# The output projection of a gated cross-attention block: one float32 matmul a product, or three in float32r

## What is computed

```python
qh, kh, vh = proj_heads(q, Wq), proj_heads(k, Wk), proj_heads(v, Wv)   # 16 heads of 64, INNER = 1024
scores = einsum('bhqd,bhkd->bhqk', qh, kh) + attn_mask
probs = softmax(scores)
ctx = einsum('bhqk,bhkd->bhqd', probs, vh).transpose(0, 2, 1, 3).reshape(b, s, -1)
attn = einsum('bse,de->bsd', ctx, Wo)                                  # the output projection
x = x + tanh(g_xattn) * attn
x = x + tanh(g_ffn) * ffn(layernorm(x))
```

## Time and profile before

| | us |
|---|---|
| median of 3 runs | 215.25 (215.03 to 215.96) |
| span of the profiled execution | 213.1 |
| TensorE matmuls busy | 198.2 (93%) |
| VectorE busy | 155.0 (73%) |
| ScalarE busy | 104.7 (49%) |
| POOL busy | 70.2 (33%) |

### The profile page before, as it was taken

The page is one execution under the profiler, slowest core; times in us unless marked ns, Lnnn a source line. Parts: engine busy times, 40 slices in busy tenths (PEclk is TensorE's granted clock), DMA queues, the critical chain, the costliest instruction groups (busy, mean ns, idle before and its releaser), DMA issues.

```text
span 213.1 us, 5086 instructions
## 1 busy us (share of the span) xinstructions
PE 198.2 (93%) x1564; PEld 172.4 (81%) x1564; DVE 155.0 (73%) x666; ACT 104.7 (49%) x352; POOL 70.2 (33%) x91
## 2 busy tenths in 40 slices
PE   7766899999989999899996999999999999999994
PEld 8564678987779877798775988888988899888894
DVE  3469998569995699956999587699665556564554
ACT  4354699467674775747757351732223232223230
POOL 3387369633036231362313610131413031230000
PEclk9999999999999999999999799999999999999999
DMA  3890000000000000020000000002202102020002
GB/s 123 288 362 7 3 14 3 12 3 14 0 0 12 0 12 0 0 62 0 0 0 6 0 0 0 5 0 77 74 0 74 59 19 74 0 74 25 0 0 98
DMA packets 5983, 7.99 MB, mean 37 GB/s; under 512 B 817, under 2 KB 3521, under 8 KB 5969
## 3 DMA queue, kind: packets, MB, share of 16 engines
q1 hardware_dynamic: 5904, 7.74, 10.8%
q0 software_dynamic: 64, 0.07, 0.2%
HBM read 7.29 MB, written 0.52 MB: 37 GB/s over the span
## 4 chain that ended last, share of the span: by engine, by line
PE 58%; DVE 21%; issue 7%; ACT 6%; DMA 3%; POOL 2%; DVEq 1%; SPq 1%; ACTq 0%
PE proj_k L397 6%; PE proj_q L397 6%; ACT probs L515 5%; PE misc L303 5%; PE o_bank L294 4%; DVE probs L690 3%; PE pt L225 3%; PE pt L227 3%; PE pt L226 3%; DMA wk_raw<-wkT 3%; PE s_even L269 3%; PE pt L279 3%; PE proj_q L225 3%; DVE rstd L745 3%; PE proj_k L225 2%
## 5 line engine op out<-in xcount | busy, mean ns | idle before, releaser
L515 ACT ACTIVATE probs<-probs,negmax 128x128 f32<-128x128 f32 x128 | 49.9, 393 | 17.6 <-DVE negmax L690 17.6
L1026 POOL TENSOR_TENSOR probs<-probs,rinv 128x512 f32<-128x512 f32 x32 | 33.0, 1042 | 58.0 <-DVE rinv L704 57.8
L592 ACT ACTIVATE silu_sb<-s_even 128x512 f32<-128x512 f32 x18 | 10.8, 598 | 43.8 <-PE s_odd L227 43.8
L515 ACT ACTIVATION_READ_ACCUMULATOR probs<-probs,negmax 128x1 f32 x128 | 24.2, 189 | 0.0
L294 PE MATMUL o_bank<-probsT,v 128*64 128x128 f32 x256 | 17.5, 278 | 3.4 <-DVE probsT L708 1.9
L858 DVE TENSOR_TENSOR h_sb<-silu_sb,s_odd 128x512 f32<-128x512 f32 x18 | 12.3, 685 | 10.7 <-ACT silu_sb L592 10.6
L858 DVE TENSOR_TENSOR h_sb<-silu_sb,pt 128x512 f32<-128x512 f32 x18 | 12.4, 687 | 10.4 <-ACT silu_sb L592 10.3
L294 PEld LDWEIGHTS o_bank<-probsT,v 128*64 128x64 f32 x256 | 13.8, 136 | 7.3 <-issue 6.8
L269 PE MATMUL s_even<-kT,qT 64*128 64x128 f32 x128 | 18.4, 284 | 0.3 <-DVE negmax L690 0.2
L279 PE MATMUL pt<-ident_sb,probs 128*128 128x128 f32 x128 | 18.1, 283 | 0.7 <-POOL probs L1026 0.7
L269 PE MATMUL s_odd<-kT,qT 64*128 64x128 f32 x128 | 18.5, 285 | 0.0
(11 more groups left out here) (162 smaller groups left out, 503.4 us busy)
## 6 DMA issues: line engine op xcount, KB each, us to landing
gu_raw<-gu SPq DMA_DIRECT2D x9, 256.0 KB, 2.7
down<-down SPq DMA_DIRECT2D x9, 128.0 KB, 2.1
wk_raw<-wkT SPq DMA_DIRECT2D x2, 256.0 KB, 4.9
wq_raw<-wqT SPq DMA_DIRECT2D x2, 256.0 KB, 7.0
mask<-mask SPq DMA_DIRECT2D x8, 64.0 KB, 1.8
wv_raw<-wvT SPq DMA_DIRECT2D x2, 256.0 KB, 7.0
wo_sb<-woT SPq DMA_DIRECT2D x1, 512.0 KB, 6.8
x_sb<-x SPq DMA_DIRECT2D x1, 384.0 KB, 7.6
```

The source lines that it names most:

```text
L515: e = act.activation(probs[:, r, l, :], probs[:, r, l, :], ACT.Exp, bias=negmax[:, r, l:l + 1], scale=-1.0, accum_out=rowsum[:, r, l:l + 1])
L592: act.activation(silu_sb[:, c, :], g_bank[c][:], ACT.Silu).then_inc(silu_done, 1)
L1026: pool.tensor_tensor(quad, quad, rinv[:, r, 4 * u:4 * u + 4].unsqueeze(2).to_broadcast([P, 4, P]), ALU.mult).then_inc(norm_done, 1)
```

## The change

Two pairs of float32r tiles take the place of `oT` and, for the product, of `wo_sb`: `oT_hi` and `oT_lo`, `wo_hi` and `wo_lo`. POOL splits Wo once. ScalarE writes the rounded half of `o_bank` into `oT_hi` (`copy_o_hi`), VectorE subtracts it from the bank into `oT_lo`, and the semaphore that tells of the result comes from VectorE as before. `out_project` has three matmuls a chunk, 24 in place of 8. TensorE waits for `wo_lo` where it waited for the transfer of Wo. `copy_o_hi` has 16 places in ScalarE's program.

```diff
-        oT = sb("oT", [P, 2, 4, P])
+        oT_hi, oT_lo = sb("oT_hi", [P, 2, 4, P], F32R), sb("oT_lo", [P, 2, 4, P], F32R)
+        wo_hi, wo_lo = sb("wo_hi", [P, CHUNKS, P], F32R), sb("wo_lo", [P, CHUNKS, P], F32R)
...
                 for c in range(CHUNKS):
-                    mm = pe.matmul(misc[:, 0:P], oT[:, c // 4, c % 4, :], wo_sb[:, c, :],
-                                   start=(c == 0), stop=(c == CHUNKS - 1))
+                    hi, lo = oT_hi[:, c // 4, c % 4, :], oT_lo[:, c // 4, c % 4, :]
+                    pe.matmul(misc[:, 0:P], hi, wo_hi[:, c, :], start=(c == 0), stop=False)
+                    pe.matmul(misc[:, 0:P], hi, wo_lo[:, c, :], start=False, stop=False)
+                    mm = pe.matmul(misc[:, 0:P], lo, wo_hi[:, c, :], start=False, stop=(c == CHUNKS - 1))
                 mm.then_inc(misc_done, 1)
...
             values(0, 0, 0)
-            pe.wait_ge(in_wo, 16)
+            pe.wait_ge(wolo_ready, 1)
             pe.wait_ge(cklo_rest, 1)
...
+            def copy_o_hi(g, r):
+                act.wait_ge(o_done, g + 1)
+                act.copy(oT_hi[:, r % 2, :, :].rearrange("p c q -> p (c q)"), o_bank[:]).then_inc(ohi_ready, 1)
...
             xT_hi_part(3, range(6, B), proj_bank["q"])
+            copy_o_hi(0, 0)
             exps(2, 2, 0)
...
                 copy_q(p + 1, 0)
                 exps(g + 3, 3, 0)
+                copy_o_hi(g + 1, 1)
                 copy_q(p + 1, 1)
                 exps(g + 3, 3, 1)

                 copy_pt(g + 2, 2)
                 copy_q(p + 1, 2)
                 exps(g + 4, 0, 0)
+                copy_o_hi(g + 2, 2)
                 copy_q(p + 1, 3)
                 exps(g + 4, 0, 1)

                 copy_pt(g + 3, 3)
                 exps(g + 5, 1, 0)
                 copy_v(p + 1, 0)
+                copy_o_hi(g + 3, 3)
                 exps(g + 5, 1, 1)

                 copy_pt(g + 4, 0)
                 exps(g + 6, 2, 0)
                 copy_v(p + 1, 1)
+                copy_o_hi(g + 4, 0)
                 exps(g + 6, 2, 1)
...
             exps(15, 3, 0)
+            copy_o_hi(13, 1)
             exps(15, 3, 1)
             copy_pt(14, 2)
+            copy_o_hi(14, 2)
             copy_pt(15, 3)
+            copy_o_hi(15, 3)
             silu(0, 0)
...
             def copy_o(g, r):
-                dve.wait_ge(o_done, g + 1)
-                dve.tensor_copy(oT[:, r % 2, :, :].rearrange("p c q -> p (c q)"), o_bank[:]).then_inc(ot_ready, 1)
+                dve.wait_ge(ohi_ready, g + 1)
+                dve.tensor_tensor(oT_lo[:, r % 2, :, :].rearrange("p c q -> p (c q)"), o_bank[:],
+                                  oT_hi[:, r % 2, :, :].rearrange("p c q -> p (c q)").bitcast(F32),
+                                  ALU.subtract).then_inc(ot_ready, 1)
...
             normalise(0, 0)
+            pool.wait_ge(in_wo, 16)
+            pool.tensor_copy(wo_hi[:], wo_sb[:]).then_inc(wohi_ready, 1)
             normalise(1, 1)
+            pool.wait_ge(wohi_ready, 1)
+            pool.tensor_tensor(wo_lo[:], wo_sb[:], wo_hi[:].bitcast(F32), ALU.subtract).then_inc(wolo_ready, 1)
             split_expert(0, 0, 1)
```

More of the change, by code:

```diff
@@ L155, in build @@
         pt0_free, pt1_free = sem("pt0_free"), sem("pt1_free")
-        o_done, ot_ready = sem("o_done"), sem("ot_ready")
+        o_done, ohi_ready, ot_ready = sem("o_done"), sem("ohi_ready"), sem("ot_ready")
+        wohi_ready, wolo_ready = sem("wohi_ready"), sem("wolo_ready")
         xn2t_ready, xn2hi_ready = sem("xn2t_ready"), sem("xn2hi_ready")
```

## The result

The changed kernel is slower by 5.5%: the ratio to the kernel before is 1.0554, 95% interval 1.0483 to 1.0625. The five runs have a median of 230.09 us (225.97 to 236.14), five of the kernel before 215.03; these medians alone give 1.070. The ratio rests on two of the five runs, 225.97 and 227.15, and leaves out the three that a low granted clock lengthened most; the profiled execution, 236.14, is one of these, so I read its undisturbed pass and take its clock as a subject of its own.

What follows compares the result with a forecast made beforehand. It took TensorE to bound the kernel, nearly gapless in loop and tail. Entry 2.65, clock 0.8, three passes 6.3 and tail 1.9 make 11.65; 213.1 + 11.65 + 2.15 = 226.9 us, range 221.5 to 229.5 (its own 224.5 to 229.5).

Steps and rivals of the forecast that it cites:

- The record: Output projection on TensorE: 112 ns per float32r record, set by the weight load; 24 make 2.68 us, +0.89 a projection.
- a slow form: Rival: each 128-column float32r product in the projections is done as two records, +3.58 us a projection, 244 us; chance 0.09.
- a faster kernel: Rival: only TensorE's time counts and projection records go at 57 ns, -3.4 us over 8 projections, 211.9 us; chance 0.03.
- The rival in which the load doesn't count: Projection records at 57 ns, -0.42 us each, pause and cast waits staying: a pass +0.8, total 222.1 us; chance 0.12.
- The pass: Attention loop: first projection +0.89 and two VectorE waits of +0.6 make +2.1 us a pass, 6.3 for three.
- The wait for the cast of group g+4: Late in a pass, VectorE's copy at 84.41 becomes a subtraction that waits for ScalarE's whole cast: +0.6 us.
- The second projection: Later projection in a pass: its +0.89 us on TensorE lies beside VectorE's longer run, so adds nothing to the pass.
- The entry: Ahead of TensorE's loop: the wait for wo_lo from POOL idles TensorE 3.3 us and delays the scores, +2.65 us.
- The clock's term: Behind the pause at the loop's start: a fall to 1.2 GHz may or may not come; 0.8 us, bounds 0 and 1.7.
- The tail: After the loop: two dearer projections on TensorE and ScalarE's cast ahead of the first silu, side by side, +1.9 us.
- The time around the span: Outside the profiled span of 213.1 us: 2.15 us, from the timed runs' median of 215.25, added at the end.

Runs made afterwards that it cites:

- f32_product: The changed kernel with one float32 matmul a chunk in place of three float32r ones, casts, subtractions and waits kept: 223.34 us, ratio 1.0417.
- half_weights: The changed kernel with only the first 64 token columns of oT_hi and oT_lo as stationary operand: 221.4 us in its one run.
- only_wo: The kernel before with POOL's split of Wo and TensorE's wait for it added, the halves unused: 219.9 us, ratio 1.0215.
- changed_again: The changed kernel run once more, unaltered, for its clock: six runs, median 227.44 us, ratio 1.0592.
- half_moving: The changed kernel with only the first 64 of Wo's columns moving, all 128 stationary columns kept: records still 112 ns; no total time given.
- late_wait: The changed kernel with TensorE's wait for wo_lo moved from ahead of the loop into out_project, ahead of its matmuls: 228.46 us, ratio 1.0621.
- the runs at 0.992: Two of the changed kernel's eleven runs, unaltered, named by their mean granted clock of 0.992: 225.97 and 226.69 us.
- late_and_first: The changed kernel with the wait for wo_lo in out_project and ScalarE's cast of group g+3 ahead of its copy of v: 221.53 us, ratio 1.0367.
- packed_256: The changed kernel with Wo's halves side by side: 16 float32r records of 256 moving columns a projection, not 24: median 224.35 us, ratio 1.0448.

## Why the prediction was right, and where it was off

**The record** was right at its forecast of 112 ns and 2.68 us a projection, and for the reason given, as far as the load can be told from the output's partitions: half the weights made it 62 ns, half the moving columns changed nothing. The Trainium skill, "TensorE: Matmul & The Clock Gate", LDWEIGHTS, would have a load of 64 columns at an estimated 53 ns, of 128 at 107; the starts of 62 and 112 are 5 to 9 ns above and agree with its rule that the columns of the stationary operand set it. The four passes that the Trainium skill, "FP8 and Floating Point Precision", TensorE Precision Notes, counts for a true float32 product don't decide here: float32r's three records took 336 ns a chunk against float32's 224. The rivals of a slow form and of a faster kernel fall with the 192 records at 112 ns. The rival in which the load doesn't count was wrong as a forecast and near as a price: with cheap records its 222.1 was measured as 221.4 in one run, and the pass as 27.7, 0.8 over the one before. So even records at that pace leave the change a loss.

**The pass** was forecast at +2.1 and measured at 28.96 less 26.88, +2.08. Its terms were less good than their sum: I had 0.89 for the projections and 1.2 for the casts; f32_product and half_weights divide it into 0.84 for the casts and 1.24 for the projections. The wait for the cast of group g+4 is 0.31 with short projections and 0.55 with long ones, so part of what I put down to ScalarE is TensorE's. The second projection, which I had put beside VectorE's run at no cost, costs 0.35 (1.24 less the first one's 0.89). That the sum came out at 2.1 all the same is luck.

**The entry** was forecast at +2.65 and, for the clock, 0.8. The pause is 3.30 us as forecast; with the fall late, in f32_product, the scores of group 3 are 7.39 us behind those of group 2, before they were 4.58: 2.8. The clock's term is the one that was mis-sized. I left open whether a fall would come; it came in eight profiles of eight. By its runs only_wo puts the entry at 4.6 us in all (interval 2.8 to 6.4), 2 us for the clock, and by its profile, with a fall of 6.8 us, at 5.4.

**The tail** was forecast at +1.9. From the scores of group 15 to the end are 101.2 us before (213.1 less 111.9) and 103.4 in changed_again (227.2 less 123.8), each with one fall of 3.4 us in it: +2.2.

**The time around the span** I took as 2.15 us from a median and the span of one execution. In every execution on record that has both, the time is 1.74 to 1.87 us above the span, so this term was 0.3 too high. Without any clock term the measured parts, 2.8 at the entry, 6.2 in three passes and 2.2 in the tail, make a span of 213.1 + 11.2 = 224.3; the run with the least time at 1.2 GHz has 224.1.

**What I had not forecast** is the falls in the loop, 3.1 us where one was measured. The long runs are those of low clock, so falls are why the runs spread to 236 and 238 us, past my range, and why the median of the first five, 230.09, is past it as well. Of thirteen profiles of changed kernels and experiments, four have 24 records 0.11 us apart in the second projection of a pass, 2.7 us, behind a gap of 1.0 to 1.1 us: the two of the changed kernel, half_moving and late_wait. In each of these the clock falls within such a projection or just behind it, in 6 of the 12 in all (half_moving has one more fall at 106.9, behind a first projection without such a gap). The other nine profiles, with 16 records, or with 62 ns records, or with a gap of 0.7 us or less, have none there in 27. That is one profile each, and the runs at 0.992 show that the two conditions together don't suffice. Which property of the projections counts isn't shown: f32_product has the same gap and the same distance, 128 columns in each record and 112 ns apart, and no fall in the loop; what it lacks is the third record a chunk, the float32r form and 0.9 us of length, and no run separates these. If the falls go with such projections, late_wait gave back there what it won at the entry, and late_and_first kept both; its runs' mean clocks, 0.977 to 1.0 against 0.962 to 0.970, say the same. The prediction's step "the clock" looked for a fall only behind the long pause.

The ratio forecast, 226.9 to 215.25, is 1.054; the measured ones are 1.055 and 1.059. Part of this agreement is luck: it holds for the runs that have few falls, and the errors at the entry, in the tail and around the span offset one another.

## What to carry to other kernels

Before splitting a float32 product into three float32r ones, count the weight loads: at 128 by 128 three records take the place of two, 2.68 us for 1.79. At 256 moving columns a record takes hardly longer than at 128 (0.12 us), but even packed so the projection only came level with float32, and the kernel with the casts stayed 4.5% slower. Ask of each moved copy what stands behind it in the order of both engines; giving a copy to the idler ScalarE cost 1.5%, since the exponentials behind it were what VectorE waited for. And look at the short gaps of a busy engine for a wait that stands behind unrelated work: one such move was worth 1.6%.

## What the runs showed of the hardware that I had not expected

The granted clock fell not only behind a pause of 3.3 us but, in half of the cases profiled, within or just behind a projection of 24 records 112 ns apart that followed a gap of 1.0 to 1.1 us (TensorE was busy 2.40 of the 3.40 us ahead of the fall at 86.1). With the same gap and 16 records, of 256 moving columns in packed_256 and of 128 in f32_product, it stayed at 1.00 in the loop. The Trainium skill, "TensorE: Matmul & The Clock Gate", HAM oscillation, ties falls to long idle gaps; the gaps here were short, and the measurement decides: a short gap doesn't rule a fall out. What besides the gap brings it about isn't shown.
